# Solve stage of a gated block: T turned once and B = T u^T in place of A and A u^T, rows of the Gram matrix multiplied where they were copied

## The reference

```python
u = k / (norm(k) + EPS)
Au = A @ u
denom = 1 + u @ Au
A = A - outer(Au, Au) / denom
z = Au / denom
M = M + outer(v, (k @ q) * z)
o = M @ q
```

## Time and profile before

| | |
|---|---|
| median of 3 runs | 1076.78 us (1076.72 to 1078.22) |
| profiled execution, its own time | 1076.09 us |
| its span, first to last instruction | 1074.4 us |
| TensorE busy | 927.1 us, 86% |
| VectorE busy | 787.6 us, 73% |
| ScalarE busy | 543.4 us, 51% |
| GpSimd busy | 301.3 us, 28% |
| mean granted TensorE clock | 0.928 |

### The profile page before, as it was taken

The page is one execution under the profiler, slowest core; times in us unless marked ns, Lnnn a source line. Parts: engine busy times, 40 slices in busy tenths (PEclk is TensorE's granted clock), DMA queues, the critical chain, the costliest instruction groups (busy, mean ns, idle before and its releaser), DMA issues.

```text
span 1074.4 us, 28516 instructions
## 1 busy us (share of the span) xinstructions
PE 927.1 (86%) x11675; PEld 715.0 (67%) x11675; DVE 787.6 (73%) x2503; ACT 543.4 (51%) x1096; POOL 301.3 (28%) x256
## 2 busy tenths in 40 slices
PE   3799999999998778587996828665899999999998
PEld 1467777777785657476894627464677777777766
DVE  6878787878679998896579779793666666665663
ACT  4678787878745344222244312100366565565574
POOL 4354444444311000000000000002756446446340
PEclk9999999999999798689999868786999999999999
DMA  5343548465437462145351000266425324334131
GB/s 153 75 106 111 139 127 202 133 135 132 119 127 223 134 164 52 30 130 129 109 159 49 5 3 4 76 153 172 100 78 109 99 70 111 97 83 115 40 79 59
DMA packets 179334, 112.47 MB, mean 105 GB/s; under 512 B 79616, under 2 KB 172160, under 8 KB 178560
## 3 DMA queue, kind: packets, MB, share of 16 engines
q1 hardware_dynamic: 162304, 93.81, 34.7%
q10 hardware_dynamic: 16896, 16.78, 5.1%
HBM read 49.16 MB, written 37.75 MB: 81 GB/s over the span
## 4 chain that ended last, share of the span: by engine, by line
PE 33%; DVE 15%; issue 1%; DMA 1%; POOL 1%; ACT 1%; SPq 0%; DVEq 0%; ACTq 0%; POOLq 0%
PE ldl_work L2044 10%; PE ldl_work L2032 10%; DVE lane_rows L1156 6%; DVE ldl_rank_one L1153 4%; PE ldl_work L2016 2%; PE ldl_work L1611 2%; DVE ldl_lane_dinv L1138 2%; PE ldl_work L1621 1%; PE ldl_work L1999 1%; PE ldl_work L2007 1%; PE ldl_work L2000 1%; PE ldl_work L1986 1%; DVE lane_rows L1134 1%; DVE lane_rows L1132 1%; PE ldl_work L1428 1%
## 5 line engine op out<-in xcount | busy, mean ns | idle before, releaser
L1797 POOL TENSOR_TENSOR T<-T,out_bv_rows 128x512 f32<-128x512 f32 x16 | 20.4, 1273 | 410.4 <-DMA out_bv_rows<-in_bqkv 404.2
L446 DVE TENSOR_TENSOR ffn_h_rest<-ffn_ps_h,ffn_h_high 128x512 f16<-128x512 f32 x128 | 86.2, 685 | 56.1 <-ACT ffn_ps_h L619 55.6
L618 ACT ACTIVATE ffn_h_high<-ffn_ps_h,b_columns 128x512 f16<-128x512 f32 x128 | 87.9, 687 | 64.6 <-PE ffn_ps_h L697 64.1
L2044 PE MATMUL ldl_work<-w_ternary,ldl_panels 128*128 128x256 f16 x512 | 118.2, 273 | 0.0
L711 PE MATMUL ffn_ps_y<-w_ternary,ffn_h_high 128*128 128x256 f16 x512 | 117.8, 273 | 0.0
L711 PE MATMUL ffn_ps_y<-w_ternary,ffn_h_rest 128*128 128x256 f16 x512 | 117.8, 272 | 0.0
L697 PE MATMUL ffn_ps_h<-ffn_xT_high,w_ternary 128*128 128x512 f16 x256 | 98.7, 386 | 11.8 <-DVE ffn_h_rest L446 11.8
L697 PE MATMUL ffn_ps_h<-ffn_xT_rest,w_ternary 128*128 128x512 f16 x256 | 98.3, 384 | 0.0
L2032 PE MATMUL ldl_work<-out_xT_high,w_ternary 128*128 128x512 f16 x256 | 97.0, 379 | 0.0
L2032 PE MATMUL ldl_work<-out_xT_rest,w_ternary 128*128 128x512 f16 x256 | 97.0, 379 | 0.0
L1945 ACT ACTIVATE ldl_work<-ldl_work,b_columns 128x512 f32<-128x512 f32 x128 | 84.2, 658 | 0.0
(11 more groups left out here) (215 smaller groups left out, 2296.4 us busy)
## 6 DMA issues: line engine op xcount, KB each, us to landing
ffn_x<-in_x SPq DMA_DIRECT2D x16, 512.0 KB, 4.7
x_scratch<-ffn_x_out ACTq DMA_DIRECT2D x16, 512.0 KB, 3.3
aT_scratch<-ffn_aT SPq DMA_DIRECT2D x16, 512.0 KB, 5.2
inv_aT<-aT_scratch SPq DMA_DIRECT2D x16, 512.0 KB, 5.1
ldl_panels<-uT_scratch SPq DMA_DIRECT2D x32, 256.0 KB, 3.1
T<-x_scratch SPq DMA_DIRECT2D x16, 512.0 KB, 3.8
uT_scratch<-ffn_uT SPq DMA_DIRECT2D x16, 256.0 KB, 5.3
inv_uT<-uT_scratch SPq DMA_DIRECT2D x16, 256.0 KB, 4.2
```

The costliest lines, as they stand in the source:

```text
L446: nc.vector.tensor_tensor(hl[n % 2][:, f], ps_h[f % 3][:], hh[n % 2][:, f], ALU.subtract).then_inc(hl_done, 1)
L618: nc.scalar.activation(hh[n % 2][:, f], ps_h[f % 3][:], ACT.Gelu, bias=c.b1[:, f:f + 1])
L2044: ins = nc.tensor.matmul(ps_y[t % 2], part[k % 2][:, f, t * P:(t + 1) * P], c.w2[:, f], start=(f == 0 and part is hh), stop=(f == FC - 1 a ...
```

## The change

`gram`: TensorE turns T (64 transposes by the identity) and ScalarE copies T^T into `m.W`. From it and u the first 32 columns of B = T u^T are made; VectorE copies them into `m.KK` and also writes them multiplied by D^-1 into `first_over_d`, which lies in the place of the right side's panel. The first diagonal block is (D^-1 B)^T B. In the second pass the other 96 columns of B are made into `m.KK` by ScalarE, and GpSimd writes D^-1 B of these columns over `m.W`. The products A and the turns of u A are gone.

`factorise`, second call: every `inject` of rows of the Gram matrix or of u A becomes `multiply`, 64 products of 32 rows: (D^-1 B)^T B for the Gram matrix and (D^-1 B)^T T for the right side. T is thus read until the last panel, so YR of r = 0 to 2 has a tensor of its own, `done_right`; buffers of the output stage (x5, xn, its two f16 parts and their transposes) are laid over it. SyncE waits for GpSimd's 16 multiplications ahead of `keep_d(0)`, TensorE ahead of `diagonal(1)`.

```diff
+        done_right = sb("done_right", [P, NW - 1, NQ, P])
+        YR = [done_right[:, k] for k in range(NW - 1)] + [m.T[:, NQ * (NW - 1):]]
-        YR = [m.T[:, NQ * k:NQ * (k + 1)] for k in range(NW)]
...
         def keep_d(r):
             sp.wait_ge(turned, r + 1)
+            if not first and r == 0:
+                sp.wait_ge(e.products.over_d, NG)
...
+        def multiply(work, r, right, dst, alone):
+            i, seen = None, set()
+            for p, q in tile_order():
+                n = NQ * q + p
+                left = e.products.first_over_d[:, n] if r == 0 else m.W[:, n, block_of(r)]
+                start = (p // 4, q) not in seen
+                seen.add((p // 4, q))
+                i = nc.tensor.matmul(work[rows_of(q), p, dst], left, right(n), start=start, stop=alone,
+                                     skip_group_check=True)
+            return i
...
-                i = inject(work, r, m.W, every, every, r == 0)
+                i = multiply(work, r, lambda n: m.T[:, n], every, r == 0)
...
-                    i = inject(work, r, m.KK, after(r), after(r), r == 0)
+                        i = multiply(work, r, lambda n: m.KK[:, n, after(r)], after(r), r == 0)
...
-            i = inject(work, r, m.KK, block_of(r), slice(0, W), r == 0)
+                pe.wait_ge(e.products.over_d, NG)
+                multiply(work, r, lambda n: m.KK[:, n, block_of(r)], slice(0, W), False)
...
                 if before < NG:
-                    sp.wait_ge(W_diag, before + 1)
+                    sp.wait_ge(b_done, before + 1)
...
     def vector(v):
+        for n in range(NG):
+            v.wait_ge(b_done, n + 1)
+            nc.vector.tensor_copy(m.KK[:, pairs(n), 0:W], ps_b[n % 2][:, :, 0:W])
+            nc.vector.tensor_tensor(first_over_d[:, pairs(n)], ps_b[n % 2][:, :, 0:W],
+                                    m.dinv[:, pairs(n)].unsqueeze(2).to_broadcast([P, GROUP, W]),
+                                    ALU.mult).then_inc(B_done, 1)
+
+    def scalar(act):
+        for n in range(NG):
+            act.wait_ge(t_done, n + 1)
+            nc.scalar.activation(m.W[:, pairs(n)], ps_t[n % 2], ACT.Copy).then_inc(Tt_done, 1)
+        for n in range(NG):
+            act.wait_ge(g_done, n + 1)
+            nc.scalar.activation(m.KK[:, pairs(n), rest], ps_t[n % 2][:, :, rest], ACT.Copy).then_inc(kk_done, 1)
+    def gpsimd(pool):
+        for n in range(NG):
+            pool.wait_ge(kk_done, n + 1)
+            nc.gpsimd.tensor_tensor(m.W[:, pairs(n), rest], m.KK[:, pairs(n), rest],
+                                    m.dinv[:, pairs(n)].unsqueeze(2).to_broadcast([P, GROUP, P - W]),
+                                    ALU.mult).then_inc(over_d, 1)
+
+    def tensor(pe):
+        def turn(n):
+            if n > 1:
+                pe.wait_ge(Tt_done, n - 1)
+            for k in range(GROUP):
+                i = nc.tensor.transpose(ps_t[n % 2][:, k], m.T[:, GROUP * n + k], c.ident[:])
+            i.then_inc(t_done, 1)
+
+        def first_columns(n):
+            pe.wait_ge(u_in[n % NU], 16 * (n // NU + 1))
+            pe.wait_ge(Tt_done, n + 1)
+            if n > 1:
+                pe.wait_ge(B_done, n - 1)
+            for k in range(GROUP):
+                i = nc.tensor.matmul(ps_b[n % 2][:, k, 0:W], m.W[:, GROUP * n + k], uT[n % NU][:, k, 0:W],
+                                     start=True, stop=True)
+            i.then_inc(b_done, 1)
...
+        e.inject_units(0, 0, True)
+        turn(0)
+        turn(1)
         for n in range(NG):
             if n + 2 < NG:
+                turn(n + 2)
+            first_columns(n)
             if n:
                 first_block(n - 1)
         first_block(NG - 1)
...
     def tensor_rest(pe):
...
+                i = nc.tensor.matmul(ps_t[n % 2][:, k, rest], m.W[:, GROUP * n + k], uT[x % NU][:, k, rest],
                                      start=True, stop=True)
...
             def _(pool):
+                solution.products.gpsimd(pool)
                 outputs.gpsimd(pool)
```

More of the change, by code:

```diff
@@ L1390, in panel @@
                 if r < NW - 1:
-                    i = inject(work, r, m.KK, after(r), after(r), r == 0)
+                    if first:
+                        i = inject(work, r, m.KK, after(r), after(r), r == 0)
+                    else:
+                        i = multiply(work, r, lambda n: m.KK[:, n, after(r)], after(r), r == 0)
                 emptied_of(pe, r, "done")
@@ L1399, in diagonal @@
             work = area(r, "diagonal")
-            i = inject(work, r, m.KK, block_of(r), slice(0, W), r == 0)
-            if not first:
+            if first:
+                i = inject(work, r, m.KK, block_of(r), slice(0, W), r == 0)
+            else:
+                pe.wait_ge(e.products.over_d, NG)
+                multiply(work, r, lambda n: m.KK[:, n, block_of(r)], slice(0, W), False)
                 inject_units(turn_number[r, "diagonal"] % 2, r, False)
@@ L1560, in vector @@
     def vector(v):
-        def scale(n):
-            if n > 1:
-                v.wait_ge(a_done, n - 1)
-            nc.vector.tensor_tensor(Td[n % 2], m.T[:, pairs(n)],
-                                    m.dinv[:, pairs(n)].unsqueeze(2).to_broadcast(group),
-                                    ALU.mult).then_inc(td_done, 1)
-        def copy_w(n):
-            v.wait_ge(w_done, n + 1)
-            if n < NG - 1:
-                nc.vector.tensor_copy(m.T[:, pairs(n)], ps_w[n % 2]).then_inc(W_done, 1)
-            else:
-                for cols in (slice(0, W), rest):
-                    nc.vector.tensor_copy(m.T[:, pairs(n), cols], ps_w[n % 2][:, :, cols]).then_inc(W_done, 1)
@@ L1612, in inverse @@
                                      start=True, stop=True)
-            i.then_inc(a_done, 1)
-        def times_u(n):
-            pe.wait_ge(u_in[n % NU], 16 * (n // NU + 1))
-            pe.wait_ge(A_done, n + 1)
-            if n > 1:
-                pe.wait_ge(W_done, n - 1)
-            for k in range(GROUP):
-                i = nc.tensor.matmul(ps_w[n % 2][:, k], A[n % 2][:, k], uT[n % NU][:, k], start=True, stop=True)
-            i.then_inc(w_done, 1)
+            i.then_inc(b_done, 1)
@@ L1644, in tensor_rest @@
     def tensor_rest(pe):
-        def columns(n):
+        for n in range(NG):
             x = NG + n
             pe.wait_ge(u_in[x % NU], 16 * (x // NU + 1))
-            if n == 0:
-                pe.wait_ge(W_done, NG + 1)
-            if n > 1:
+            if n < 2:
+                pe.wait_ge(Tt_done, NG)
+            else:
                 pe.wait_ge(kk_done, n - 1)
             for k in range(GROUP):
-                i = nc.tensor.matmul(ps_g[n % 2][:, k, rest], uT[x % NU][:, k], m.T[:, GROUP * n + k, rest],
+                i = nc.tensor.matmul(ps_t[n % 2][:, k, rest], m.W[:, GROUP * n + k], uT[x % NU][:, k, rest],
                                      start=True, stop=True)
             i.then_inc(g_done, 1)
-        def turn(n):
-            if n > 1:
-                pe.wait_ge(UA_done, n - 1)
-            for k in range(GROUP):
-                i = nc.tensor.transpose(ps_u[n % 2][:, k], m.T[:, GROUP * n + k], c.ident[:])
-            i.then_inc(u_done, 1)
-        for n in range(NG):
-            columns(n)
-            turn(n)
         pe.wait_ge(kk_done, NG)
-        pe.wait_ge(UA_done, NG)
     e.first_blocks, e.all_blocks = W_diag, NG
     o = Names()
-    o.sync, o.vector, o.scalar, o.tensor, o.tensor_rest = sync, vector, scalar, tensor, tensor_rest
+    o.first_over_d, o.over_d = first_over_d, over_d
+    o.sync, o.vector, o.scalar, o.tensor, o.tensor_rest, o.gpsimd = sync, vector, scalar, tensor, tensor_rest, gpsimd
     return o
@@ L1707, in outputs_feed_forward @@
     rstd = sb("rstd", [P, BT])
-    xn = sb("xn", [P, BT, D])[:]
-    xh = sb("xn_high", [P, BT, D], F16)
-    xl = sb("xn_rest", [P, BT, D], F16)
-    xTh = [sb(f"xT_high{s}", [P, BT, DC, P], F16) for s in range(2)]
-    xTl = [sb(f"xT_rest{s}", [P, BT, DC, P], F16) for s in range(2)]
+    xn = place(0, 0)
+    xh, xl = (place(1, 0)[:, 2 * s:2 * s + 2].bitcast(F16).rearrange("p a (t d) -> p (a t) d", t=2) for s in range(2))
+    xTh, xTl = ([y[:, 2 * s:2 * s + 2].bitcast(F16).rearrange("p a (t d x) -> p (a t) d x", t=2, d=DC) for s in range(2)]
+                for y in (place(1, 1), place(2, 0)))
     hh = [y[:].bitcast(F16).rearrange("p (f a) x -> p f (a x)", f=FC) for y in (e.Z, e.ZR)]
```

59 lines of the change are left out of this document (15 added, 44 removed).

## The result

The kernel after took 1093.97 us (median of 4 runs, 1086.71 to 1106.29), the one before beside it 1076.75 us (1075.93 to 1078.22): slower, 1.0132 times, interval 1.0098 to 1.0167. Forecast was 1075.3 us. The ratios here leave out single runs more than 1.5% above the fastest of their kernel (1106.29 us above), but a run with a smaller loss to the clock stays in.

The account below looks back on a forecast made before the run. TensorE's products to 552 us, then VectorE's four leaves, bound the changed stretch. Stage -7.0, port +5.5 and multiplying 0 gave -1.5 us on 1076.78: forecast 1075.3 us, own range 1072.5 to 1078.5, wider range 1069.3 to 1079.5.

Parts of the forecast that it names:

- The stage ahead of leaf 0: TensorE's products from 516.17 to 551.98 us get shorter, groups of 1.85 us, leaf 0 starting near 545 us: -7.0 us.
- Rival (d): Stage's 32-column products cost other than 0.88 us: 1071.3 us (chance 0.07) or 1078.3 us (0.04).
- The shared port: In leaf 0, GpSimd's 16 multiplications make VectorE's two-tensor operations stand still: +5.5 us.
- (a): Rival in leaf 0: GpSimd costs the leaf nothing, 1069.8 us; chance 0.15.
- (b): Rival in leaf 0: port at full price, leaf longer by 12.8 us, 1082.6 us; chance 0.07.
- Multiplying in place of moving: Beside the leaves, ten injections of 32 instructions become ten products of 128, hidden by the leaves: 0 us.
- the cover: Behind leaf 2, three products' +4.7 us are hidden in TensorE's 6.93 us of idle time, 2.2 us left.
- rival (c): Behind leaf 2, weights can't load while neighbours run: 46 ns each, TensorE 4.0 us late, 1079.3 us; chance 0.07.
- The end: Last leaf: one product of 3.4 to 3.8 us precedes the issues of W's rows, not what outputs first wait for.

Follow-up runs that it names:

- g1: f1 with two products of 128x512 added in TensorE's stop ahead of the first product with u: 1084.24 us, ratio 1.0057.
- f3: Kernel after, with e2's edit and the stores of W's rows waiting only for the last product that reads W: 1077.78 us, ratio 0.9991.
- e2: Kernel after, with D^-1 B of the other 96 columns by 64 ScalarE activations in place of GpSimd's 16 multiplications: 1085.97 us, ratio 1.0057.
- e0: Kernel after, unchanged, run and profiled again: 1095.35 us, ratio 1.0125.
- e3: Kernel before, with each row injection of the solve split into 128 instructions in place of 32, nothing multiplied: 1090.85 us, ratio 1.0125.
- f2: Kernel before, with the 32 products of 512 columns beside leaf 2 made twice: 1080.1 us, ratio 1.0006.
- g2: f3 with the first two loads of u in the other order, so TensorE stands longer before the stage's first product with u: 1097.56 us.
- f4: f3 with the columns for diagonal 3 and panel 2 multiplied beside leaf 0, then moved by 32 products each beside leaf 2: 1095.73 us.
- f1: Kernel after, with the stores of W's rows waiting only for the last product that reads W, not the last subtraction: 1103.06 us.

## Why the prediction was wrong

Of the prediction's terms the stage and the port held. Two that it put at nothing, the multiplications and the end, cost some 5 us each, and the clock, which it left out, cost 19 us in some of the runs. The clock isn't the whole of it: the fastest runs of the kernel after, 1086.71 and 1087.26 us, are 10 us above the one before as well.

**The stage ahead of leaf 0, -7.0 us: right in mechanism and size, where the clock held.** It was -7.8 to -8.8 us (g1, f3, e2, e0). Groups of 1.77 us (forecast 1.85), first take at 543.33 us (near 545). From the first of the eight products with 32 columns to the next instructions are 0.90 us (517.32 to 518.22), for 0.88 forecast and some 0.17 of gap behind it; a turn is 0.50 for 0.44. Rival (d) is out.

**What the step left out: the clock.** The prediction took every duration at the clock of the row that it came from. In the profiles of the kernel before, of e3 and of f2, whose stage is made of products with 128 columns for the most part, it takes 40.4 to 40.9 us; the change leaves a stream of short products that, once the clock has fallen, doesn't bring it back, and it then costs 19 us (51.4 to 51.8 for 32.0 to 33.1). g1 and g2 point to the stop ahead of the first product; g1 is the stronger, and neither shows it alone. The prediction said of that product that it "is held by the load of u, which is issued at the same place afterwards", and so priced the stop at nothing. The row it names gives ScalarE's copy as what ended the 0.64 us, not the load; it is only after the change that the load ends it.

**The shared port, +5.5 us: right, measured 6.0**, and gone with e2. The rule of the Trainium skill ("SBUF — State Buffer", Who interferes with whom) that the prediction names agrees with this trace: two-tensor instructions contend, and in both directions. L1160 at 567.06 loses 0.47 of the 0.60 us that GpSimd still had to run, so it stands still but for its first 0.13 us, less than the 0.24 that the prediction allowed for. The leaf loses 6.0 / 16 = 0.37 us per GpSimd instruction and not 0.83; a part of the waiting is GpSimd's, whose 1.18 us are 0.35 more than it takes alone. Rivals (a) and (b) are out.

**Multiplying in place of moving, 0 us: wrong by 5 to 6 us.** The failed step is the cover, "+4.7 us against 6.93 us idle. Hidden, with 2.2 us left": it adds up the products' own times as though instructions were there when they are wanted. Those times were not too low: 128 products with 32 columns take 1.67 us, 13 ns each, against the 30 ns taken "whatever the width" and the 46 ns of rival (c), 128 with 128 columns 32 ns each at full clock (62 in 1.95 us, kernel after, 717.75 us), and the three beside leaf 2 come to +1.7 us, not +4.7. But 288 more of them beside leaf 2 (384 for 96), in front of the 384 narrow ones of the next diagonal, have to be fetched, and the fetch gives 128 with their weights in 3.5 us. Rival (c) had the right place and nearly the right effect (4.0 us) by a wrong mechanism: weights don't wait for their neighbours. e3 makes the lateness with no arithmetic, f4 takes it away by count, and f2, with more added product time than the change but few instructions, makes 2.5 us of it, for 4.8 us in the kernel after and 6.1 in e3. f2 also shows that the 6.93 us of idle time that I counted as cover can't be spent without loss; that they are used for fetching is my reading of it.
The Trainium skill ("Runtime: NRT & Kernel Launch", Instruction fetch mechanics) says that instructions come in blocks of 256, and that crossing from one to the next is mostly hidden. The trace agrees with the 256 (128 products and their weights from stop to stop) and disagrees with hidden: 1.35 to 2.18 us at each, where such a block is worked off in 1.51 us.

**The end, "their end is not what the output stage waits for first": wrong, by 5 us.** The output stage's first transpose does wait for the last four rows only, but these and D^-1 stand behind the twelve stores on SyncE's queue (e2 and f3 above), and between D^-1 and the last rows SyncE waits until all that was stored before has landed. In the kernel after:

```profile
SPq L1747 <- DMA dinv<-ldl_dinv_turned: 4.2, 1, 4.2
```

Before it was 1.4 us, in f3 2.6. With this wait the last rows are issued 10.6 us after D^-1 is turned for 7.9 before, and the first transpose follows 5.3 us later for 3.2, right behind loads that waited for the same landing; why it is 5.3 isn't shown. I had named the issues and priced nothing. The stores go 4 us later against the last leaf, behind the stop of 3.08 us, and the end goes with them; let go earlier, it is 13.1 us (f1), 12.6 (g1) and 11.9 us (f3) for 11.05 before. In e0 half a clock adds another 11 us.

**The sum of a run with the clock in full**, g1: 1.9 (begins later) - 7.8 + 6.0 + 6.8 (between leaves) + 1.5 (rows early) + 1.8 (outputs) = 10.2 us, and its span is 10.2 us longer. For the kernel after, 1.8 + 10.5 + 6.0 + 4.8 + 4.8 + 2.3 = 30.2 us. Why the stage begins between 0.3 us earlier and 1.9 us later, and why the outputs take 332.6 to 335.2 us in kernels that don't differ there, stays open; so does what decides in a single run whether the clock falls.

## What to carry to other kernels

When an edit turns few wide TensorE instructions into many narrow ones, count instructions and not their time: past 128 products in a row that take less than 27 ns each the supply sets the pace, and idle time ahead of a burst is where it seems to catch up. Look for stops released by "issue" in the trace before, hidden ones too. Look for every stop of TensorE ahead of a long stretch of narrow products: here a stop of 0.8 us or more went with half the clock for all of it, and two wide products put into the stop kept five runs of five, by their times, clear of it. Release a store by the last instruction that reads the place it writes over, not by the end of the job around it.

## What the runs showed of the hardware

- With short products TensorE stops at every 128 of them or sooner, with a transfer of instructions of 17 KB some 3 us ahead of the end of each stop; from stop's end to stop's end are 3.3 to 3.7 us, of which 128 products run for 1.5 us.
- Products with weights of 128x32, four column groups in turn, cost 13 ns each with 32 columns (1.67 us for 128) where no stop falls into them.
- A clock that had fallen to 0.50 stayed there for 26 us (e0) and 47 us (after, 521 to 568 us) of unbroken work with 32 to 128 moving columns.
- VectorE and GpSimd, both with two operands in SBUF, slow each other: a GpSimd instruction takes 1.18 us for 0.83, and the leaf 0.37 us more for each.
